# Cross-attentions: transposed probabilities kept in 32 bits, one product per head with v

## The reference, cut to what matters

```python
Q = (query @ Wq + bq).reshape(B, Lq, NUM_HEADS, D_K).transpose(0, 2, 1, 3)
K = (key @ Wk + bk).reshape(B, Lk, NUM_HEADS, D_K).transpose(0, 2, 1, 3)
V = (value @ Wv + bv).reshape(B, Lk, NUM_HEADS, D_K).transpose(0, 2, 1, 3)
scores = jnp.einsum('bhqd,bhkd->bhqk', Q, K) / SCALE
scores = jnp.where(m, -jnp.inf, scores)
...
attn = jax.nn.softmax(scores, axis=-1)
...
out = jnp.einsum('bhqk,bhkd->bhqd', attn, V)
out = out.transpose(0, 2, 1, 3).reshape(B, Lq, D_MODEL)
return out @ Wo + bo
...
x = x + jnp.tanh(g_xattn[0]) * _L0_xattn_ref(_layernorm(x, axis=-1), ctx_1024, ctx_1024, ...)
```

## Time and profile before

| | us |
|---|---|
| median of 3 runs | 1442.24 |
| lowest, highest | 1440.13, 1442.91 |
| span of the profiled execution, first to last instruction | 1442.0 |
| PE busy in it | 1253.7 (87%) |
| PE's weight loads busy | 996.9 (69%) |
| DVE busy | 1135.6 (79%) |
| ACT busy | 903.7 (63%) |

### The profile page before, as it was taken

The page is one execution under the profiler, slowest core; times in us unless marked ns, Lnnn a source line. Parts: engine busy times, 40 slices in busy tenths (PEclk is TensorE's granted clock), DMA queues, the critical chain, the costliest instruction groups (busy, mean ns, idle before and its releaser), DMA issues. The chain is left out here.

```text
span 1442.0 us, 35263 instructions
## 1 busy us (share of the span) xinstructions
PE 1253.7 (87%) x13822; PEld 996.9 (69%) x13822; DVE 1135.6 (79%) x2068; ACT 903.7 (63%) x2071; POOL 278.4 (19%) x242
## 2 busy tenths in 40 slices
PE   1599998589989899889938999994699999999996
PEld 1376666367767767667725676763489999899995
DVE  5578887689999999999643777777688888888884
ACT  1477875158667677667624667663277677677762
POOL 2000000100000000000000000000236666666663
PEclk8689999799999999999666999995599999999998
DMA  8000000133452353352220000000867788778871
GB/s 231 12 9 9 6 2 2 41 93 74 114 146 67 101 151 76 100 151 73 68 66 9 5 9 5 2 2 1 290 225 227 227 249 245 222 231 250 234 189 30
DMA packets 172065, 152.96 MB, mean 106 GB/s; under 512 B 62589, under 2 KB 154386, under 8 KB 171906
## 3 DMA queue, kind: packets, MB, share of 16 engines
q1 hardware_dynamic: 151906, 129.51, 30.0%
q0 software_dynamic: 13936, 16.79, 6.1%
q10 hardware_dynamic: 6064, 4.46, 1.1%
HBM read 116.89 MB, written 36.70 MB: 107 GB/s over the span
## 5 line engine op out<-in xcount | busy, mean ns | idle before, releaser
L1857 POOL DMA_INDIRECT out<-m_yo,m_xg x70 | 161.5, 2307 | 135.9 <-DVE m_yo L1972 120.5
L1879 ACT ACTIVATE m_hf<-m_ps,m_bue 128x256 f32<-128x256 f32 x280 | 117.3, 471 | 106.5 <-PE m_ps L84 106.5
L82 PE MATMUL m_ps<-m_xt,m_us 128*128 128x256 f16 x560 | 153.7, 274 | 0.0
L83 PE MATMUL m_ps<-m_xt,m_us 128*128 128x256 f16 x560 | 153.7, 274 | 0.0
L84 PE MATMUL m_ps<-m_xt,m_us 128*128 128x256 f16 x560 | 153.6, 274 | 0.0
L82 PE MATMUL m_ps<-m_ds,m_hs 128*128 128x256 f16 x560 | 152.6, 273 | 0.3 <-DVE m_yo L1972 0.3
L84 PE MATMUL m_ps<-m_ds,m_hs 128*128 128x256 f16 x560 | 152.6, 273 | 0.0
L83 PE MATMUL m_ps<-m_ds,m_hs 128*128 128x256 f16 x560 | 152.6, 273 | 0.0
L473 ACT ACTIVATE x_pr<-x_ps,x_mx 128x120 f32<-128x120 f32 x512 | 143.3, 375 | 9.8 <-DVE x_mx L687 9.2
L1053 ACT ACTIVATE f_pr<-f_ps,f_nb 128x256 f32<-128x256 f32 x256 | 107.8, 477 | 66.0 <-DVE f_nb L1331 65.7
L481 ACT ACTIVATE x_pt<-x_ps 120x512 f16<-120x512 f32 x128 | 77.0, 602 | 86.2 <-PE x_ps L84 78.8
(11 more groups left out here) (367 smaller groups left out, 3832.7 us busy)
## 6 DMA issues: line engine op xcount, KB each, us to landing
m_uraw<-in_L_ffn_Wup SPq DMA_DIRECT2D x35, 1024.0 KB, 5.5
m_draw<-in_L_ffn_Wdown SPq DMA_DIRECT2D x35, 1024.0 KB, 5.8
head_values<-f_v_row SPq DMA_DIRECT2D x16, 520.0 KB, 5.5
f_vh<-head_values SPq DMA_DIRECT2D x16, 520.0 KB, 3.9
head_outputs<-f_at_row SPq DMA_DIRECT2D x16, 512.0 KB, 3.0
f_at_in_t<-head_outputs SPq DMA_DIRECT2D x16, 512.0 KB, 6.1
expert_values<-f_pv_row SPq DMA_DIRECT2D x8, 512.0 KB, 2.8
f_pv_in_t<-expert_values SPq DMA_DIRECT2D x8, 512.0 KB, 5.6
```

Of the source, the lines that this page charges most:

```text
L82: pe.matmul(out, lhs[0], rhs[0], start=(n == 0), stop=False)
L83: pe.matmul(out, lhs[0], rhs[1], start=False, stop=False)
L1857: pool.indirect_dma_start(rows_of, bass.IndirectOffsetOnAxis(xg[j % RING][:, ti, D:D + 1].bitcast(I32), 0), yo[j % 2][:, ti, :], None, bou ...
L1879: ins = act.activation(hf[:, q, m, :], U(q)[:, m, :], ACT.Gelu, bias=weights.bue[par][:, 2 * q + m:2 * q + m + 1], scale=UNSPLIT)
```

## The change

The transposed probabilities are copied once, in 32 bits and without scaling: by ACT in even units, by DVE in odd ones, each waiting for the transposes itself. There are two semaphores in place of two, one for each copying engine. v is one 32-bit tensor, written by a single DVE instruction from PSUM, its ones set once. Each head has one product with 32-bit operands in place of three with 16-bit ones.

```diff
-        vf = two("vf", [SK, D])
-        va = two("va", [SK, 2, H, DK + 1], F16)
+        va = two("va", [SK, H, DK + 1])
...
-        pt = two("pt", [SK, 2, HG, P], F16)
+        pt = two("pt", [SK, HG, P])
...
-        pt_hi = sem("pt_hi")
-        pt_done = sem("pt_done")
+        pt_copied = [sem("pt_by_act"), sem("pt_by_dve")]
...
             def pt_part(b, u):
+                if u % 2 == 1:
+                    return
                 n = XA_UNITS * b + u
                 act.wait_ge(pt_ready, n + 1)
                 if n >= 2:
                     act.wait_ge(pv_done, n - 1)
-                act.activation(pt[u % 2][:, 0], PT(u), ACT.Copy, scale=SPLIT).then_inc(pt_hi, 1)
+                act.activation(pt[0][:], PT(u), ACT.Copy).then_inc(pt_copied[0], 1)
...
                 if n >= 2:
-                    pe.wait_ge(pt_done, n - 1)
+                    pe.wait_ge(pt_copied[u % 2], n // 2)
...
-                pe.wait_ge(pt_done, XA_UNITS * b + u + 1)
+                pe.wait_ge(pt_copied[u % 2], (XA_UNITS * b + u) // 2 + 1)
                 for h, head in enumerate(heads(u)):
-                    last = matmul3(pe, O(ti)[:, head, :],
-                                   [(tuple(pt[u % 2][:, hl, h, :] for hl in range(2)),
-                                     tuple(va[b % 2][:, hl, head, :] for hl in range(2)))])
+                    last = pe.matmul(O(ti)[:, head, :], pt[u % 2][:, h, :], va[b % 2][:, head, :], start=True, stop=True)
...
-                    chain(dve.scalar_tensor_tensor(vf[par][:], front[0:SK, 0:D], 1.0 / SPLIT, s.bv[0:SK, layer, :],
-                                                   ALU.mult, ALU.add))
-                    v = vf[par][:].rearrange("k (h d) -> k h d", h=H)
-                    chain(dve.tensor_copy(va[par][:, 0, :, 0:DK], v))
-                    dve.tensor_tensor(va[par][:, 1, :, 0:DK], v, va[par][:, 0, :, 0:DK], ALU.subtract).then_inc(front_done, 1)
+                    by_head = lambda ap: ap.rearrange("k (h d) -> k h d", h=H)
+                    dve.scalar_tensor_tensor(va[par][:, :, 0:DK], by_head(front[0:SK, 0:D]), 1.0 / SPLIT,
+                                             by_head(s.bv[0:SK, layer, :]), ALU.mult, ALU.add).then_inc(front_done, 1)
...
             def pt_part(b, u):
-                dve.wait_ge(pt_hi, XA_UNITS * b + u + 1)
-                dve.scalar_tensor_tensor(pt[u % 2][:, 1], PT(u), SPLIT, pt[u % 2][:, 0],
-                                         ALU.mult, ALU.subtract).then_inc(pt_done, 1)
+                if u % 2 == 0:
+                    return
+                n = XA_UNITS * b + u
+                dve.wait_ge(pt_ready, n + 1)
+                if n >= 2:
+                    dve.wait_ge(pv_done, n - 1)
+                dve.tensor_copy(pt[1][:], PT(u)).then_inc(pt_copied[1], 1)
```

More of the change, by code:

```diff
@@ L424, in _ @@
             if layer == 1:
-                sp.wait_ge(ones_set, 6)
+                sp.wait_ge(ones_set, 4)
                 sp.dma_start(s.rows_in[0:1, :], zeros[0:1, :]).then_inc(rows_zeroed, 16)
@@ L432, in _ @@
             for par in range(2):
-                chain(pool.memset(va[par][:, 0, :, DK:DK + 1], 1.0))
-                chain(pool.memset(va[par][:, 1, :, DK:DK + 1], 0.0))
+                chain(pool.memset(va[par][:, :, DK:DK + 1], 1.0))
             chain(pool.memset(zeros[:], 0.0))
@@ L595, in _ @@
                 project(0, j)
-            pe.wait_ge(ones_set, 4)
+            pe.wait_ge(ones_set, 2)
             score(0, 0)
```

## The result

The change made the kernel slower: 1533.7 us against 1442.5 (medians), a ratio of 1.063 with a 95% interval of 1.060 to 1.065. One of the changed kernel's four executions took 1559.6 us at a mean granted clock of 0.872, against 0.894 to 0.898 in the others, and is left out of the ratio. The profiled execution took 1533.05 us, its span is 1531.3, 89.3 more than before.

What follows compares the result with a forecast made beforehand. PE's list was taken as the bound, fully in layer 1 and nearly in layer 0. From 1442.0 us, 39.0 for layer 1, 29.4 for layer 0, -1.2 at stage ends (67 together) and 15 for the clock gave 1524, range 1458 to 1610.

Steps and rivals of the forecast that it cites:

- PE is the bound, and no one waits for the copies: Both cross-attentions: PE's list bounds layer 1 and nearly layer 0, where relieving DVE and ACT returns at most 1.48 us a batch.
- Copies at 602 and 689 ns, the new wait at nothing: Probability copies cost 602 ns on ACT, 689 on DVE; DVE's wait for PE's transposes, in place of ACT, costs nothing.
- Two passes a product, 115 ns apart: Each head's 32-bit product takes two passes, spaced 115 ns apart by their weight loads: 185 ns recorded less 70 overlapping.
- 0.61 us more a unit: PE's products with v: eight passes take 0.92 us a unit in place of 0.31, 39.0 us over each layer's 64 units.
- the 1.2 us that I gave them: Layer 0: longer products fill 1.2 of PE's 1.48 us of waits a batch, 9.6 us, leaving 29.4 of 39.0.
- The clock, 15 us: Layer 0: PE loses its upper clock level for 30 us at half speed, 15 us lost; bounds nothing to 160 us.
- the sign of being wrong in this term: Clock term in layer 0: wrong if the upper level shows throughout or the lower one for more than 60 us.
- the two large terms: PE's longer 32-bit products with v, 0.61 us more a unit in both layers, and layer 0's lost clock level, 15 us.
- the level holds: Rival for layer 0: PE's upper clock level isn't lost, so the total is 1509 us; chance 0.22.

Runs made afterwards that it cites:

- the relief alone: One 16-bit copy per unit, by ACT and DVE in turn, three 16-bit products per head kept, against the kernel before: 1433.2 us, ratio 0.993.
- both shapes: The changed kernel with 34 columns streamed in half the passes, 1505.8 us, and with each head's product cut into two of 64 queries, 1471.2 us.
- The dense filler: The changed kernel with one overwritten product of 480 columns ahead of each unit's scores in layer 0: 1507.5 us, ratio 1.045 to the kernel before.
- thin filler: The changed kernel with eight overwritten products of 17 columns ahead of each unit's scores in layer 0: 1559.2 us, ratio 1.082 to the kernel before.

## Why the prediction was right

- *PE is the bound, and no one waits for the copies.* Right in layer 1 to the hundredth: with the relief alone its batch stays at 25.14. In layer 0 the relief returns 0.97 us a batch; I had put an upper bound of 1.48 on it and counted nothing.
- *Copies at 602 and 689 ns, the new wait at nothing.* Right: 602 and 691, DVE and ACT at 16.0 and 15.4 us a batch (I had about 15), and PE doesn't wait for `x_pt`.
- *Two passes a product, 115 ns apart.* Right: 1024 passes, 111 ns. I took the 185 ns of line 1670 less the 70 that overlap; the record is 192, and both shapes show that the load sets the pace. The Trainium skill ("TensorE: Matmul & The Clock Gate", section "LDWEIGHTS (loading the stationary operand)") gave 107, which is as near to the measured 111 from the other side.
- *0.61 us more a unit.* Too much. I counted eight loads where seven count, since the first runs beneath the transposes: 0.81 against 0.31. In layer 1 a steady batch gives (28.92 - 25.14) / 8 = 0.47, or 30 us for 64 units where I had 39; 27 came, since the first batch grew by only 1.2 us (28.03 to 29.26). In layer 0 it is 2.36 a batch, 19 us for 29. PE's idle time there shrinks from 1.5 to 0.3 us a batch, but not for the reason that I gave. The relief alone takes 0.97 from the batch, and the product then adds 3.33 (24.67 - 21.34) where layer 1 has 3.78. So the longer products filled some 0.45 of the 1.2 us that I gave them, and the relief more than made up for the rest.
- *The clock, 15 us.* This term was mis-sized, the other way. At the lower level were 82 to 110, which takes in part of the second batch (30.7), parts of two later batches that took 30 in place of 24.7, and all of the stage from 263 on. That is more than the 60 us that I had named as the sign of being wrong in this term. Layer 1 begins 62.4 us late; 19 of it are the price at the upper level, and some 43 are left. The dense filler bears this out: with it layer 1 begins at 798.1 in place of 832.5, although the filler adds 1.4 us to each batch of layer 0. My ground for the small end was that the level hadn't moved once from 82 to 242. But that was work with short 16-bit products; the rows couldn't say how near to a fall it was.

So the mechanisms of the two large terms were right and their sizes weren't. That the sum (1524) is near the result is luck: two errors, 22 us too much and 28 too little, nearly cancel. The case "the level holds" (1509) is close to what one gets when it is held by filler (1507), and that is luck as well: the 1509 has the 22 us too much in it, the 1507 some 11 us of filler.

## What to carry to other kernels

Read what one more instruction costs on the engine that is busy all through a batch, before what it saves on others: taking about a seventh of the work from DVE and ACT (18.73 to 16.03 and 17.66 to 15.33 us a batch) returned 9 us. Against that run, one wider operand type on PE cost 3.3 us a batch in layer 0 and 3.8 in layer 1 at the upper level, some 57 in all, and the lost level some 43 more. A 32-bit product with few columns (17 and 34 here) is priced by its two loads of the stationary operand, not by what it streams. And where PE's clock is granted by level, a slower mix of instructions can be paid for twice, by its length and by the level that it loses; a run with dense filler and one with thin filler of the same length tell that apart from a mere lack of work.

## What the runs showed that I had not expected

- Loads of 64 columns for the two halves of a head's queries overlap: pairs every 58 ns, against 111 for one load of 128 columns of the same data.
- PE busy for all of 36.8 us stood at 0.50 throughout (263 to 300 after the change), with no wait of PE in them. A full PE isn't a sign of the upper level.
- The changed kernel and its variant with wider products have the same batches at the upper level (24.67 and 28.92), and yet took 1533 and 1506 in one execution each: in the first the level fell three times in layer 0 between 170 and 270, in the second not at all.
